# First block of a recommender tower: gather and scratch by halves, loads on two queues, layer 1's weights behind the first products

## What is computed

```
x0 = stack(tbl_f[ids[:, f]] for f in 32 fields)                # (1024, 32, 64)
out = relu(einsum(W0, h * x0 over all pairs of fields) + b0)   # h = x0: 32 x 32 pairs, 128 outputs
h, final0 = out[:, :64], out[:, 64:]
final1 = relu(einsum(W1, h * x0 over all pairs) + b1)          # 64 x 32 pairs, 128 outputs
z = sum over the 64 columns of (final0, final1)
y = relu(relu([z, dense] @ W_top1 + b) @ W_top2 + b) @ W_top3
```

## Time and profile before

| | us |
|---|---|
| median of 3 runs | 2001.28 (1998.69 to 2001.33) |
| profiled execution, its own time | 2000.27 |
| its span, first to last instruction | 1998.4 |
| PE busy | 1951.9 (98%) |
| DVE busy | 1913.1 (96%) |
| POOL busy | 1804.2 (90%) |
| ACT busy | 1711.2 (86%) |

### The profile page before, as it was taken

The page is one execution under the profiler, slowest core; times in us unless marked ns, Lnnn a source line. Parts: engine busy times, 40 slices in busy tenths (PEclk is TensorE's granted clock), DMA queues, the critical chain, the costliest instruction groups (busy, mean ns, idle before and its releaser), DMA issues.

```text
span 1998.4 us, 28527 instructions
## 1 busy us (share of the span) xinstructions
PE 1951.9 (98%) x7176; PEld 1342.8 (67%) x7176; DVE 1913.1 (96%) x1230; ACT 1711.2 (86%) x1943; POOL 1804.2 (90%) x708
## 2 busy tenths in 40 slices
PE   2999999999999999999999999999999999999998
PEld 1677677667666666666666766776776676676664
DVE  3999999999999999999999999999999999999991
ACT  2889898888889889889889888888888888888883
POOL 3999999999999999999999999999999999999881
PEclk9999999999999999999999999999999999999999
DMA  7988888888788888788788788888888887887820
GB/s 190 216 209 194 185 188 195 183 189 193 183 190 193 182 191 195 178 193 194 179 194 192 182 193 190 185 193 186 188 193 183 190 194 180 192 194 179 192 67 0
DMA packets 268304, 364.13 MB, mean 182 GB/s; under 512 B 107505, under 2 KB 107889, under 8 KB 268162
## 3 DMA queue, kind: packets, MB, share of 16 engines
q1 hardware_dynamic: 258338, 352.61, 77.0%
q0 software_dynamic: 8192, 8.40, 1.7%
q10 hardware_dynamic: 1760, 2.96, 0.5%
HBM read 347.02 MB, written 16.78 MB: 182 GB/s over the span
## 4 chain that ended last, share of the span: by engine, by line
PE 91%; POOL 5%; issue 2%; SPq 1%; DMA 1%; ACT 0%; DVE 0%; POOLq 0%
PE out L636 60%; PE out L618 20%; PE out L626 8%; POOL zl L221 4%; PE out L620 1%; SPq L263 0%; PE out L683 0%; DMA fields_dram<-emb 0%; POOL emb L204 0%; PE hrep L683 0%; SPq L288 0%; SPq L273 0%; PE out L676 0%; PE z L676 0%; PE hrep L676 0%
## 5 line engine op out<-in xcount | busy, mean ns | idle before, releaser
L221 POOL TENSOR_TENSOR zl<-prod,zh 128x2048 fp32r<-128x2048 f32 (+2 forms) x384 | 1545.6, 4055 | 68.8 <-ACT zh L376 51.5
L636 PE MATMUL out<-zh,w1h 128*128 128x512 f32 x1856 | 757.2, 408 | 5.5 <-DVE zl L517 3.9
L636 PE MATMUL out<-zl,w1h 128*128 128x512 f32 x1856 | 725.5, 391 | 0.0
L636 PE MATMUL out<-zh,w1l 128*128 128x512 f32 x1856 | 724.6, 390 | 0.0
L376 ACT ACTIVATE zh<-prod 128x2048 fp32r<-128x2048 f32 (+2 forms) x384 | 652.5, 1699 | 69.3 <-DVE prod L562 44.4
L389 ACT ACTIVATE hrep<-out,b_sb 32x512 f32<-32x512 f32 (+1 forms) x768 | 495.2, 645 | 90.7 <-PE out L620 80.9
L618 PE MATMUL out<-prod,w_sb 128*128 128x512 f32 x1024 | 465.3, 597 | 35.0 <-DVE prod L500 30.1
L636 PEld LDWEIGHTS out<-zh,w1h 128*128 128x128 f32 x1856 | 348.8, 188 | 174.1 <-POOL zl L221 61.0
L636 PEld LDWEIGHTS out<-zh,w1l 128*128 128x128 f32 x1856 | 349.4, 188 | 75.9 <-issue 3.5
L636 PEld LDWEIGHTS out<-zl,w1h 128*128 128x128 f32 x1856 | 349.0, 188 | 76.1
L618 PEld LDWEIGHTS out<-prod,w_sb 128*128 128x128 f32 x1024 | 195.3, 191 | 232.5 <-issue 222.7
(11 more groups left out here) (61 smaller groups left out, 696.2 us busy)
## 6 DMA issues: line engine op xcount, KB each, us to landing
rot_low<-fields_dram SPq DMA_DIRECT2D x512, 256.0 KB
rot_high<-fields_dram SPq DMA_DIRECT2D x512, 256.0 KB
xrep<-fields_dram SPq DMA_DIRECT2D x256, 128.0 KB
fields_dram<-emb SPq DMA_DIRECT2D x512, 32.0 KB, 5.2
left_x<-fields_dram SPq DMA_DIRECT2D x256, 64.0 KB, 2.4
left_y<-fields_dram SPq DMA_DIRECT2D x256, 64.0 KB, 2.2
emb<-in_tables,idx POOLq DMA_INDIRECT x256
w_sb<-in_w ACTq DMA_DIRECT2D x1, 1024.0 KB
```

Source lines behind the costliest of these rows:

```text
L221: pool.tensor_tensor(zl[u][:, 0:size, :], product[:, 0:size, :], zh[u][:, 0:size, :].bitcast(F32), ALU.subtract).then_inc(zl_made[u], 1)
L636: mm = nc.tensor.matmul(out1[:, :], w[:, k, :], z[:, t, :], start=start and t == 0 and part == 0, stop=stop and t == size - 1 and part == 2)
```

## The change

Block 0 is handled apart from the other blocks, by halves of 8 rows:

- Its ids and table offsets come in a small tensor of their own (`ids_first`, 128 x 6), first on SP's queue. POOL gathers the two tiles of half 0, then the two of half 1, on semaphores of their own.
- Each gathered tile is written to the scratch by two transfers (`write_first`): the first tile of each half by SP, the second by ACT. SP loads `rot_low` of step 0 after half 0 is written (`first_written`); ACT loads `xrep` by halves (`load_first_xrep`), and `left_x`; SP loads `left_y`.
- Block 1's scratch write is shared by SP (two groups) and ACT (two), and stands ahead of `rot_low1` and `rot_high0`. Block 2's stands ahead of `rot_low2` and all that follows. `rot_high1` moves behind block 1's `xrep` and `left` loads.
- W1 is loaded by ACT after its half 0 scratch writes; ACT rounds it and DVE takes the remainder behind the products of step 0.
- Step 0's products are made in two instructions, each with a semaphore, so that PE's first two tiles wait on the first alone.
- Behind layer 0 of step 0, `replicate_h1` stands ahead of `finish_l0`. In ACT's step 0, `copy_x(2)` and `copy_left(1)` stand behind `replicate_h0(1)` and `round_split(0, 2)`.

```diff
+HGATHERS = GATHERS // HALVES
+HGROUP = P // SROWS
+GATHERED_APART = 16 * HGATHERS
+WRITTEN_APART = 16 * 2 * HGATHERS
...
+        def written(b, nth):
+            return nth * WRITTEN - (WRITTEN_APART if b == 0 else 0)
+
+        def write_first(queue, half, g, written):
+            for c in range(2):
+                row = c * FIELDS + g * HGROUP
+                queue.dma_start(
+                    fields_dram[row:row + HGROUP, half * SC:(half + 1) * SC].rearrange("f (r d) -> f r d", d=DIM),
+                    emb[0][:, half * HGATHERS + g, :]).then_inc(written, 16)
+
+        def write_groups(queue, n, b, groups):
+            for g in groups:
+                for c in range(2):
+                    row = c * FIELDS + g * GROUP
+                    queue.dma_start(
+                        fields_dram[row:row + GROUP, bass.ds(n * COLS, COLS)].rearrange("f (r d) -> r f d", d=DIM),
+                        emb[b][:, g, :]).then_inc(scratch_written[b], 16)
+
+        def load_first_xrep(queue, half, loaded):
+            for q in QUAD_ORDER:
+                queue.dma_start(xrep[q * FIELDS:(q + 1) * FIELDS, half * SC:(half + 1) * SC],
+                                fields_dram[0:FIELDS, half * SC:(half + 1) * SC]).then_inc(loaded, 16)
...
+            pool.wait_ge(ids_first_loaded, 16)
+            pool.tensor_tensor(idx[0][:, :].rearrange("p (h g) -> p h g", g=HGATHERS),
+                               ids_first_sb[:, 0:GATHERS].rearrange("p (h g) -> p h g", g=HGATHERS),
+                               ids_first_sb[:, GATHERS:].unsqueeze(1).broadcast_to([P, HALVES, HGATHERS]),
+                               ALU.add).then_inc(idx_made, 1)
+            pool.wait_ge(idx_made, 1)
+            for g in range(HGATHERS):
+                gather_first(0, g, first_gathered[g])
+            for g in range(HGATHERS):
+                gather_first(1, g, gathered[0])
             pool.wait_ge(ids_loaded, 32)
-            for n in range(AHEAD):
+            for n in range(1, AHEAD):
                 if n >= 2:
-                    pool.wait_ge(scratch_written[n % 2], WRITTEN)
+                    pool.wait_ge(first_written, WRITTEN_APART)
+                    pool.wait_ge(scratch_written[0], written(0, 1))
...
+            sp.dma_start(ids_first_sb[:, :], ids_first).then_inc(ids_first_loaded, 16)
             sp.dma_start(ids_sb[:, :], ids).then_inc(ids_loaded, 16)
             sp.dma_start(first_row_sb[:, :], first_row).then_inc(ids_loaded, 16)
-            write_scratch(0, 0, 1)
-            sp.wait_ge(scratch_written[0], WRITTEN)
-            load_xrep(0)
+            sp.wait_ge(first_gathered[0], 16)
+            write_first(sp, 0, 0, first_written)
+            sp.wait_ge(gathered[0], GATHERED_APART)
+            write_first(sp, 1, 0, scratch_written[0])
+            sp.wait_ge(first_written, WRITTEN_APART)
             load_low(0, 0)
-            load_left(0, left_x, 0, left_x_loaded)
-            load_left(0, left_y, LEFT, left_y_loaded)
+            sp.wait_ge(scratch_written[0], written(0, 1))
+            load_left(sp, 0, left_y, LEFT, left_y_loaded)
+            sp.wait_ge(gathered[1], 16 * GATHERS)
+            write_groups(sp, 1, 1, (0, 1))
             load_low(1, 1)
             load_high(0, 0)
-            write_scratch(1, 1, 1)
-            load_high(1, 1)
+            write_scratch(2, 0, 2)
             sp.wait_ge(scratch_written[1], WRITTEN)
+            load_low(2, 2)
             sp.wait_ge(xr_copied, 2)
             load_xrep(1)
             sp.wait_ge(left_copied, 1)
-            load_left(1, left_x, 0, left_x_loaded)
+            load_left(sp, 1, left_x, 0, left_x_loaded)
             sp.wait_ge(left_made, 1)
-            load_left(1, left_y, LEFT, left_y_loaded)
-            load_low(2, 2)
+            load_left(sp, 1, left_y, LEFT, left_y_loaded)
+            load_high(1, 1)
             load_low(3, 3)
-            write_scratch(2, 0, 2)
...
+                if known(m) and m == 0:
+                    act.wait_ge(first_xrep_loaded, 16 * QUADS)
+                elif known(m) and m == 1:
+                    act.wait_ge(xrep_loaded, 16 * QUADS)
...
+                first = known(m) and m == 0
+                if not first and is_up_to(i, c, LAST - 2):
                     copy_x(m + 2, b)
-                if b == 0 and is_up_to(i, c, LAST - 2):
+                if not first and b == 0 and is_up_to(i, c, LAST - 2):
                     copy_left(i * 2 + (c + 2) // 2)
                 round_split(m, 0, in_parts(0, b), p1_made, prod[1])
                 round_split(m, 3, in_parts(3, b), z4_made[0], z4)
@@ -420,7 +477,11 @@
                 round_split(m, 1, in_parts(1, b), p2_made, prod[2])
                 if is_up_to(i, c, LAST - 1):
                     replicate_h0(m + 1)
+                if first:
+                    copy_x(2, 0)
                 round_split(m, 2, in_parts(2, b), p3_made, prod[3])
+                if first:
+                    copy_left(1)
...
-            act.dma_start(w1_sb[:, :, :], w1).then_inc(w1_loaded, 16)
             act.wait_ge(w0_folded, 4)
             act.activation(w0l_parts[:, :, :], w0l_sb[:, :, :], ACT.Copy).then_inc(w0l_rounded, 1)
+            act.wait_ge(first_gathered[1], 16)
+            write_first(act, 0, 1, first_written)
+            act.dma_start(w1_sb[:, :, :], w1).then_inc(w1_loaded, 16)
+            act.wait_ge(gathered[0], GATHERED_APART)
+            write_first(act, 1, 1, scratch_written[0])
+            act.wait_ge(first_written, WRITTEN_APART)
+            load_first_xrep(act, 0, first_xrep_loaded)
+            act.wait_ge(scratch_written[0], written(0, 1))
+            load_left(act, 0, left_x, 0, left_x_loaded)
+            act.wait_ge(gathered[1], 16 * GATHERS)
+            write_groups(act, 1, 1, (2, 3))
+            copy_x(0, 0)
+            load_first_xrep(act, 1, xrep_loaded)
+            copy_left(0)
+            round_left(0)
             act.wait_ge(w1_loaded, 16)
             for u in range(PARTS):
                 act.activation(w1h[:, FIRST[u]:FIRST[u] + SIZES[u], :], w1_sb[:, SPLITS[u], :],
                                ACT.Copy).then_inc(w1_rounded, 1)
+            copy_x(1, 1)
             act.wait_ge(bias_loaded, 32)
-            copy_x(0, 0)
-            copy_left(0)
-            copy_x(1, 1)
-            round_left(0)
             replicate_h0(0)
+            replicate_h1(0)
             finish_l0(0, 0, 0)
-            replicate_h1(0)
...
+                if known(m) and m == 0:
+                    for half, made in ((slice(0, 2), first_x_made), (slice(2, LOW), x_made)):
+                        nc.vector.tensor_tensor(prod[0][:, half, :], repeated(xr, 2), rot_low[c][:, half, :],
+                                                ALU.mult).then_inc(made, 1)
...
+            products_l0(0, 0, 1)
+            left_products(0)
+            left_low(0)
             for u in range(PARTS):
                 part = slice(FIRST[u], FIRST[u] + SIZES[u])
                 dve.wait_ge(w1_rounded, u + 1)
                 nc.vector.tensor_tensor(w1l[:, part, :], w1_sb[:, SPLITS[u], :], w1h[:, part, :].bitcast(F32),
                                         ALU.subtract).then_inc(w1_split, 1)
-            products_l0(0, 0, 1)
-            left_products(0)
-            left_low(0)
...
+                first = known(m) and m == 0
+                if first:
+                    pe.wait_ge(first_x_made, 1)
```

60 lines of the change are left out of this document (36 added, 24 removed).

## The result

The changed kernel takes 1988.34 us, median of 4 runs (1987.74 to 1988.63); the kernel before took 1999.99 in the same session (4 runs, 1998.15 to 2001.33; with three of them its median was 2001.28, from which the forecast starts). The ratio is 0.9941, interval 0.9927 to 0.9955. The profiled span is 1985.9 us for 1998.4. The forecast was 1989.8, range 1986.0 to 1996.0; of the 1.5 between it and the measured median, 1.3 is that starting point. (A line number L700 is that of the changed kernel; its L414 is `copy_x`, L420 `copy_left`, L432 `zh`, L445 `replicate`, L462 `finish_l0`, L574 the halved first product, L700 layer 0.)

A forecast was written before the change was run, and what follows sets the result against it. PE, busy 98% of the span, was taken to bound the kernel, leaving only the start to win. The 12.3 us lead at step 2, less 0.5, rounded down to 11.5, gave 2001.28 - 11.5 = 1989.8 us, range 1986.0 to 1996.0.

The forecast's parts named there:

- 12.3 of lead: Step 2: the transfers hold it until 65.5, leaving it 12.3 us earlier, a lead carried through the even bodies.
- the first product: Block 0's start: first product near 21.6 for 27.65, PE's first matmul at 22.9 for 30.09, 7.2 us earlier.
- (d): Rival, loop: a new phase between PE, POOL and ACT lengthens the period, 0.3 a body giving 2007.8 us; chance 0.04.
- the 0.5 taken off for PE's lead over POOL: Loop: part of the 1.0 of PE's lead over POOL may be gone, so 0.5 us less gain.
- The stall on ACT: ACT's step 0: `zh0` no longer stands behind `copy_x(2)`, at 34.7 for 47.73, 13.0 us earlier.
- (c): Rival, ACT: within 0.2%, the stall only moves to `copy_x(2)` ahead of `zh2`, 3.5 us left, 1997.8; chance 0.11.
- a sign of being wrong: Block 0's start: the prediction counts as wrong if the first product waits beyond 24.
- four `left_x` and four writes: ACT's queue at the start: these issue from 15.3 at no more than 0.65 each, to 20.5, a copy to 21.1.
- I lean to the upper one: PE before step 2's layer 0: at 2.4 GHz it stands at 51.5, 15.3 us earlier; otherwise 13.0.
- they hold step 2 until 65.5: Block 2's `left_x` lands at 65.5, 6.3 us earlier than before, while compute wants it at 62.5 to 64.8.
- Rival (b): Step 2: transfers don't hold it, as writes and gathers cost less; 13.5 to 15.3 less, 1986 to 1987.8; chance 0.11.
- rival (a): Start: transfers gain less, W1 at 236 GB/s, first product 4.2 earlier; 1991.3 to 1995.3 us, middle 1993; chance 0.28.

The follow-up runs named there:

- e1_copy_first: Changed kernel with `copy_x(0)` ahead of ACT's four writes of block 1; PE starts at 23.55, 2.6 earlier, with no gain in the end.
- e5_both_first: Changed kernel with the second `xrep` load and `copy_x(0)` ahead of ACT's wait for block 1's gathers; PE's layer 0 of a late step 0.7 earlier.
- e12_no_w1_load: Changed kernel without W1's load, weights filled with a constant by VectorE; PE's layer 0 of a late step 1.05 earlier.
- e4_act_order_back: Changed kernel with ACT's step 0 in the old order, `copy_x(2)` and `copy_left(1)` ahead of `zh0`; PE's layer 0 of a late step 6.5 later.
- e3_w1_early: Changed kernel with W1's load back at the start of ACT's queue, its split still behind the products; PE's layer 0 of a late step 0.5 earlier.
- e9_orders_without_halves: Kernel before with ACT's new order and SP's new load order for blocks 1 and 2, without halved gathers or moved weights; 2.6 of lead.
- e6_low4_behind: e5_both_first with `rot_low4` issued behind block 2's x and left rows in SP's order; ratio 0.9937 to the kernel before.
- e7_keep_clock: e6_low4_behind with extra products on TensorE, 7 ahead of the first group and 4 between the first two; 1986.17 us, ratio 0.9934.
- e2_act_order_only: Kernel before with only ACT's step 0 reordered, `copy_x(2)` and `copy_left(1)` behind `replicate_h0(1)` and `round_split(0, 2)`; 3.0 of lead.

## Why the prediction was right, and where it was not

**The total.** 12.3 of lead were forecast at step 2 and 12.3 measured (54.52 for 66.81); 12.5 in the late row; the median is 11.65 lower, forecast 11.5. That the two 12.3 are alike is luck: the forecast had the engines 13.0 to 15.3 earlier and let the transfers cut this to 12.3, while in the run the engines themselves won 12.3, since the first product came out short, and the transfers cut nothing. The bodies keep their period, so (d) did not happen, and the 0.5 taken off for PE's lead over POOL didn't show. The stall on ACT did not move on (`copy_x(2)` at 44.14 has no wait), so (c) did not happen.

**The first product was mis-sized.** It was put at 21.6, and PE 7.2 earlier; it came at 24.75, with PE 4.0 earlier. That is beyond 24, which the prediction itself had named as a sign of being wrong. Up to SP's issue of `rot_low0` all was right or better (11.58 for 12.7). What failed is the sentence that ACT's "four `left_x` and four writes" are issued from 15.3 at 0.65 each: the four writes belong to block 1, and wait for its gathers. The prediction gave that wait no time; with a flight like the earlier trace rows's 2.5 it would have been over before 17. It took until 21.24, 8.2 after the last issue, beside full transfers, and the four writes behind it held the copy until 24.11. e1_copy_first shows that this was the difference (copy at 21.55, forecast 21.1), and that undoing it for the first copy alone wins nothing, since the second half of `xrep` then lands at 32.25 behind the same gathers. Together, in e5_both_first, they are worth 2.6 at the second group (34.60, where 34.7 was forecast). e12_no_w1_load shows that W1's load isn't what slows the gathers: without it they land 0.9 earlier, as much as they scatter.

**The stall on ACT** was the largest real part: 10.7 earlier at `zh0` (37.05 for 47.73), forecast 13.0. Of these 4.7 come from the earlier second group and 6.0 from the order itself; e4_act_order_back measures 6.5 at the end for that order.

**The clock.** From POOL's first remainder to step 2's layer 0 it took 17.1 us before and 15.5 after: 1.6 more lead, where "I lean to the upper one" gave 2.3. Before, the granted clock is 0.50 from 54 to 58 while PE works off these products; in the changed kernel it is 1.00. e4_act_order_back, with a shorter stretch at the low clock, takes 15.5 as well, so no run gives the clock's price by itself. So the lead at step 2 is 4.7 + 6.0 + 1.6 = 12.3.

**The transfers.** That they hold step 2 until 65.5 named a bound that is real, but it didn't bind here: copies at 64.96 and 65.50 without a wait. With less time lost before, it binds (0.86 to 65.13 in e3_w1_early, 0.72 to 64.55 in e5_both_first). The two limits lie within half a microsecond of each other, which made the forecast's mistake invisible in the total. Rival (b) thus had the right mechanism for the changed kernel (the transfers don't hold it), with a smaller lead of compute; rival (a)'s first product of 4.2 less was nearly the measured one, but not by W1's price. The Trainium skill's rule that queues of all engines share the 16 DMA engines ("DMA: Bandwidth & Descriptors", section "Issuing engines are not separate DMA queues") agrees with the trace. From 16 to 22 us, with two queues, the share is 1.06 to 1.07 at 230 to 254 GB/s; one queue had 1.07 and 236 from 22 us on the earlier trace rows. The second queue brought issue slots, no bandwidth.

**The parts are not additive.** ACT's order alone is worth 3.0, everything else alone 6.0 (e4_act_order_back), both 12.5. The halves, with the early ids, the second queue, the halved product and W1's split behind the products, bring 10.4 on top of both orders (e9_orders_without_halves against e3_w1_early); no run takes the halved gathers out alone. W1's move brings nothing (0.5 the wrong way), the halved product about 1.1 at PE's start.

**A better version.** e6_low4_behind (late row 1.2 earlier, ratio 0.9937 for 0.9941) and e7_keep_clock (2.55 earlier, 0.9934) lead the changed kernel in the late row by more than its scatter, but the ratios' intervals overlap its own. What is left at the start hangs on block 1's gathers. Not tried: the order of e5_both_first with the large loads issued behind these gathers, as they are in e3_w1_early.

## What to carry to other kernels

When a wait is removed, list for each following instruction on that queue when its own data lands; twice here (e2_act_order_only, e1_copy_first) an edit did exactly what it was for, and the next late load took the gain. A lead that one engine shows at the start need not last in a steady loop: here POOL's row near 83 us told the late row's lead to 0.4 us, and PE's at step 2 was up to 1.0 off. Compare a fixed instruction late in the loop, not the span, where the tail has a clock of its own.
